# Three-layer graph network, one core: built blocks and one-hots moved inside the windows of layers 1 and 2, the dense tiles of layer 3 on two banks, the self edge put into the blocks

## The reference

```python
loops = jnp.arange(n)
src = concatenate([src, loops]); dst = concatenate([dst, loops])
norm_edge = dinv[src] * dinv[dst]
for W, b in ((W1, b1), (W2, b2), (W3, b3)):
    h = relu(segment_sum((h @ W)[src] * norm_edge[:, None], dst) + b)
x = layernorm(x + h)
```

## Time and profile before

| what | us |
|---|---|
| median of 3 runs | 2859.15 (2855.75 to 2860.95) |
| the profiled execution's own time | 2853.73 |
| its span, first to last instruction | 2851.4 |
| PE busy | 2381.7 |
| POOL busy | 1900.6 |
| DVE busy | 1013.9 |
| ACT busy | 539.5 |

### The profile page before, as it was taken

The page is one execution under the profiler, slowest core; times in us unless marked ns, Lnnn a source line. Parts: engine busy times, 40 slices in busy tenths (PEclk is TensorE's granted clock), DMA queues, the critical chain, the costliest instruction groups (busy, mean ns, idle before and its releaser), DMA issues.

```text
span 2851.4 us, 37925 instructions
## 1 busy us (share of the span) xinstructions
PE 2381.7 (84%) x11284; PEld 1529.4 (54%) x11285; DVE 1013.9 (36%) x1370; ACT 539.5 (19%) x1322; POOL 1900.6 (67%) x1996
## 2 busy tenths in 40 slices
PE   7887777777777778888888888888988898989897
PEld 6754555555555555443443434343446677777676
DVE  8733434444344343332222222222222323232322
ACT  6412332333333323221101111111110000000000
POOL 4377776777777776767777777777776555555543
PEclk9799999999999999999999999999998999999898
DMA  6344545554554554877777777777775545454543
GB/s 188 126 120 145 165 145 157 162 162 149 166 163 138 168 162 138 255 231 230 231 227 232 226 232 228 231 228 229 231 224 183 170 144 179 139 182 139 176 133 100
DMA packets 195418, 515.59 MB, mean 181 GB/s; under 512 B 39468, under 2 KB 87203, under 8 KB 189251
## 3 DMA queue, kind: packets, MB, share of 16 engines
q0 software_dynamic: 120240, 362.54, 43.6%
q1 hardware_dynamic: 69171, 111.99, 11.6%
q10 hardware_dynamic: 5984, 40.77, 3.9%
HBM read 444.05 MB, written 71.09 MB: 181 GB/s over the span
## 4 chain that ended last, share of the span: by engine, by line
PE 49%; POOL 17%; issue 14%; DMA 9%; DVE 5%; POOLq 3%; ACT 1%; DVEq 0%; ACTq 0%; SPq 0%
PE ps_acc L1229 21%; POOL rows L559 17%; PE ps_T L1298 15%; DMA rows<-table,idx 9%; PE ps_o L1265 6%; POOLq L568 3%; PE ps_acc L1227 2%; DVE works L893 1%; PE ps_d L1174 1%; PE ps_e L1286 1%; PE ps_l L1286 1%; DVE acc L827 1%; PE ps_h L1252 1%; PE ps_d L1252 1%; ACT parts L1088 1%
## 5 line engine op out<-in xcount | busy, mean ns | idle before, releaser
L559 POOL DMA_INDIRECT rows<-table,idx x1955 | 1855.2, 949 | 839.0 <-issue 703.2
L1229 PE MATMUL ps_acc<-rows,sel 128*128 128x256 f32 (+2 forms) x3948 | 1455.6, 486 | 314.1 <-DMA rows<-table,idx 220.4
L1229 PEld LDWEIGHTS ps_acc<-rows,sel 128*128 128x128 f32 x3948 | 689.4, 197 | 774.0 <-DMA rows<-table,idx 379.5
L827 DVE TENSOR_TENSOR acc<-ps_acc,acc 128x256 f32<-128x256 f32 (+1 forms) x123 | 65.3, 531 | 1119.2 <-PE ps_acc L1229 1119.2
L746 DVE SCALAR_TENSOR_TENSOR sel<-ps_e,firsts,dstT 128x1152 f32<-128x1152 f32 x242 | 342.7, 1416 | 0.0
L1265 PE MATMUL ps_o<-w,hT 128*128 128x512 f32 (+1 forms) x784 | 270.5, 488 | 0.8 <-ACT hT L1051 0.8
L745 DVE COPY idx<-srcT 128x9 int32 (+1 forms) x242 | 45.7, 189 | 634.0 <-PE ps_acc L1229 631.4
L1298 PE MATMUL ps_T<-parts,rows 128*128 128x256 bf16 x1764 | 240.2, 285 | 25.9 <-DVE agg L852 25.9
L1298 PE MATMUL ps_T<-parts,works 128*128 128x256 bf16 x1764 | 234.7, 281 | 23.8 <-DVE agg L852 23.8
L1071 ACT ACTIVATE made<-ps_o,dinv 128x512 f32<-128x512 f32 (+1 forms) x98 | 56.8, 580 | 900.3 <-PE ps_o L1265 900.3
L1298 PEld LDWEIGHTS ps_T<-parts,rows 128*128 128x128 bf16 x1764 | 179.4, 102 | 81.8 <-issue 34.8
(11 more groups left out here) (174 smaller groups left out, 1303.2 us busy)
## 6 DMA issues: line engine op xcount, KB each, us to landing
built<-parts SPq DMA_DIRECT2D x24, 1568.0 KB, 6.5
rows<-table,idx POOLq DMA_INDIRECT x1955, 2.9
works<-built ACTq DMA_DIRECT2D x12, 1568.0 KB, 6.9
rows<-built ACTq DMA_DIRECT2D x12, 1568.0 KB, 6.8
table<-made SPq DMA_DIRECT2D x49, 256.0 KB
acc<-table SPq DMA_DIRECT2D x49, 256.0 KB
acc<-table SPq DMA_DIRECT2D x74, 128.0 KB
table<-parts SPq DMA_DIRECT2D x7, 896.0 KB, 8.7
```

Of the source, the lines that this page charges most:

```text
L559: pool.indirect_dma_start(out=rows_of[phase][:, k, 0:WIDTH[phase]], out_offset=None, in_=table[phase][0:nodes, :], in_offset=bass.Indirect ...
L827: v.tensor_tensor(acc[:, 0:w], ps_acc[:, 0:w], acc[:, 0:w], ALU.add).then_inc(sum_taken, 1)
L1229: ins = mm(ps_acc[:, 0:w], sel[:, k, :], first if k == 0 else rows_of[phase][:, k, 0:w], start=(k == 0), stop=(k == ORDER[-1]))
```

## The change

1. **Layer 1, DVE.** `one_hots` moves ahead of `take_sum` in the same window. The windows with one-hots are written out in groups of four.
2. **Layer 1, PE.** The eight pairs of a half move from positions 10 to 17 to positions 1 to 8, ahead of the hidden layer and the product. In the last window of layer 1 they start at position 5. The first four building windows of layer 2 take the places of the other windows of layer 2, with the product at the end.
3. **Layer 1, ACT.** Four of the eight copies of a half come right after `scale`, the other four after the turned tile's copy, all ahead of `made` (but in one window, where they stay at the end).
4. **Self edge.** DVE adds the identity to the diagonal block of each built tile in `making` (`add_self`), 24 times, and SP stores the block row after that. SP's store of a block row stands one tile later in its queue: three of them (before: two) now stand behind windows of layer 2. `take_dense`, SP's loads of the dense tiles' own rows and their semaphores are gone.
5. **Layer 3.** The dense tiles use two banks in turn, ps_T and ps_h; the normalization reads the bank itself. The 147 matmuls are spread over 18 positions instead of 17, the first six of them ahead of slot 0.

The diff, cut to its core:

```diff
-        ps_dense = ps_T
+        ps_dense = [ps_T[:, 0:C], ps_h[:, 0:C]]
...
                     def store_built(j, of):
-                        sp.wait_ge(pair_kept, 2 * PAIRS * (j + 1) + 2)
+                        sp.wait_ge(self_added, j + 1)
...
-                    def dense_rows(j, n, first=False):
-                        if not first:
-                            sp.wait_ge(acc_d_used, j)
-                        sp.dma_start(acc_d, table[2][bass.ds((GATHER + j) * P, P), :]).then_inc(own_d_in, 16)
+                    def dense_residual(j, n, first=False):
...
-                        with sp.Fori(0, (T - BUILT_FROM) // 4) as i:
+                        rows_and_store(BUILT_FROM)
+                        with sp.Fori(0, (T - BUILT_FROM) // 4 - 1) as i:
                             for b in range(4):
-                                rows_and_store(BUILT_FROM + 4 * i + b)
+                                rows_and_store(BUILT_FROM + 4 * i + b + 1)
                                 if b % 2 == 1:
                                     store_built(2 * i + b // 2, b // 2)
+                        for b in range(3):
+                            rows_and_store(T - 3 + b)
+                            if b == 1:
+                                store_built(DENSE - OVER // 2 - 2, 0)
                         store(T - 1)
                     elif phase == 1:
-                        for b in range(OVER):
+                        for b in range(OVER + 1):
                             rows_and_store(1 + b)
-                            if b % 2 == 1:
-                                store_built(DENSE - OVER // 2 + b // 2, b // 2)
-                        with sp.Fori(OVER + 1, T) as t:
+                            if b % 2 == 0:
+                                store_built(DENSE - OVER // 2 - 1 + b // 2, 1 - b // 2 % 2)
+                        with sp.Fori(OVER + 2, T) as t:
...
-            def take_dense(j):
+            def finish_dense(j, into, seq):
                 v_.wait_ge(dense_done, j + 1)
-                v_.wait_ge(own_d_in, 16 * (j + 1))
-                v.tensor_tensor(acc_d, ps_dense[:, 0:C], acc_d, ALU.add).then_inc(dense_taken, 1)
-            def finish_dense(j, seq):
-                v_.wait_ge(dense_taken, j + 2)
-                normalize(acc_d, GATHER + j, acc_d_used, j + 1, res_d, res_d_in, j, seq, y3_d, y3_d_free, y_d_ready)
+                normalize(ps_dense[into], GATHER + j, dense_taken, j + 3, res_d, res_d_in, j, seq, y3_d, y3_d_free, y_d_ready)
+            def add_self(j, of):
+                v_.wait_ge(pair_kept, 2 * PAIRS * (j + 1) + 2)
+                its = making[of][:, bass.ds(GATHER + j, 1), :].rearrange("p a d -> p (a d)")
+                v.tensor_tensor(its, its, ident[:, :], ALU.add).then_inc(self_added, 1)
...
             def one_window():
-                def steady(phase, t):
+                def steady(phase, t, hots=None, whole=None):
                     n = nth(phase, t)
                     base = base_of(t)
                     prepare(n, t, base, 0)
+                    if whole is not None:
+                        add_self(*whole)
+                    if hots is not None:
+                        one_hots(hots)
...
                 v_.wait_ge(key_kept, len(key_banks))
-                with v_.Fori(BUILT_FROM, T) as t:
-                    steady(0, t)
-                    one_hots(t - BUILT_FROM)
+                def four(i, first, phase, whole=True):
+                    for b in range(4):
+                        steady(phase, first + b, 4 * i + b,
+                               None if b % 2 or not whole and b == 0 else (2 * i + b // 2 - 1, 1 - b // 2))
+                        if phase == 1 and b > 0:
+                            split(b - 1)
+                four(0, BUILT_FROM, 0, False)
+                with v_.Fori(1, (T - BUILT_FROM) // 4) as i:
+                    four(i, BUILT_FROM + 4 * i, 0)
                 to_next(0)
-                steady(1, 1)
-                one_hots(T - BUILT_FROM)
-                with v_.Fori(2, OVER + 1) as t:
-                    steady(1, t)
-                    one_hots(T - BUILT_FROM - 1 + t)
-                    split(t - 2)
-                with v_.Fori(OVER + 1, T) as t:
+                four((T - BUILT_FROM) // 4, 1, 1)
+                steady(1, OVER + 1, None, (DENSE - 1, 1))
+                split(OVER - 1)
+                with v_.Fori(OVER + 2, T) as t:
...
                 finish(0, nth(2, 0) + 2, 0)
-                with v_.Fori(2, GATHER) as t:
+                def pair(t, into):
                     steady(2, t)
-                    take_dense(t - 2)
                     finish(t - 1, nth(2, t) + 1, of_gather(t - 1))
-                    finish_dense(t - 2, of_dense(t - 2))
+                    finish_dense(t - 2, into, of_dense(t - 2))
+                with v_.Fori(0, DENSE // 2 - 1) as i:
+                    for into in range(2):
+                        pair(2 * i + into + 2, into)
+                pair(GATHER - 1, 0)
                 n = nth(2, GATHER)
                 take_sum(2, n - 1, n - 1, True)
-                take_dense(DENSE - 1)
                 finish(GATHER - 1, n + 1, of_gather(GATHER - 1))
-                finish_dense(DENSE - 1, of_dense(DENSE - 1))
+                finish_dense(DENSE - 1, 1, of_dense(DENSE - 1))
...
-            def tile(phase, t, per):
+            def tile(phase, t, per, built_half=None, at_end=False):
                 n = nth(phase, t)
                 scale(phase, t, per)
+                def keep(*gs):
+                    if built_half is not None:
+                        keep_pairs(*built_half, range(*gs))
+                if not at_end:
+                    keep(0, PAIRS // 2)
                 if phase == 0:
                     act.wait_ge(turned, n + 1)
                     nc.scalar.activation(aggT[:, 0:C], ps_T[:, 0:C], ACT.Copy).then_inc(aggT_ready, 1)
+                    if not at_end:
+                        keep(PAIRS // 2, PAIRS)
...
                         relu_T(ps_T[:, m * P:(m + 1) * P], b2T, m)
+                    keep(PAIRS // 2, PAIRS)
                 w = WIDTH[phase + 1]
                 act.wait_ge(o_done, n + 1)
                 act.wait_ge(made_free, n + 1)
                 act.sem_inc(act_step, 1)
                 nc.scalar.activation(made[:, 0:w], ps_o[:, 0:w], ACT.Copy, scale=dinv[:, bass.ds(t, 1)]).then_inc(made_ready, 1)
+                if at_end:
+                    keep(0, PAIRS)
...
-            def keep_half(i, j, of, part):
-                for g in range(PAIRS):
+            def keep_pairs(i, j, of, part, gs):
+                for g in gs:
...
-                with act.Fori(0, (T - BUILT_FROM) // 4) as i:
+                def four(i, first, phase):
                     for b in range(4):
-                        tile(0, BUILT_FROM - 1 + 4 * i + b, 1)
-                        keep_half(4 * i + b, 2 * i + b // 2, b // 2, b % 2)
+                        tile(phase, first + b, 1, (4 * i + b, 2 * i + b // 2, b // 2, b % 2),
+                             isinstance(i, int) and phase == 0 and b == 3)
+                FOURS = (T - BUILT_FROM) // 4
+                with act.Fori(0, FOURS - 1) as i:
+                    four(i, BUILT_FROM - 1 + 4 * i, 0)
+                four(FOURS - 1, T - 5, 0)
                 tile(0, T - 1, 1)
-                for b in range(OVER):
-                    tile(1, b, 1)
-                    keep_half(2 * DENSE - OVER + b, DENSE - OVER // 2 + b // 2, b // 2, b % 2)
+                four(FOURS, 0, 1)
...
-            pe.sem_inc(dense_taken, 1)
+            pe.sem_inc(dense_taken, 2)
...
-                        ins = mm(ps_dense[:, 0:C], counts_of, parts[:, h, i, :], start=(h == 0 and i == 0),
+                        ins = mm(ps_dense[into], counts_of, parts[:, h, i, :], start=(h == 0 and i == 0),
...
-                def building(i):
+                def building(i, start=1):
                     def beside(k):
                         at = ORDER.index(k)
-                        if at >= SLOTS - PAIRS:
-                            build(i, at - (SLOTS - PAIRS))
+                        if start <= at < start + PAIRS:
+                            build(i, at - start)
                     return beside
                 def with_dense(i, into):
                     def beside(k):
                         at = ORDER.index(k)
-                        if at > 0:
-                            dense(i, into, range((at - 1) * T // (SLOTS - 1), at * T // (SLOTS - 1)))
+                        dense(i, into, range(at * T // SLOTS, (at + 1) * T // SLOTS))
...
-                steady(0, T - 1, LAST_PLACES[0], building(T - 1 - BUILT_FROM))
+                steady(0, T - 1, LAST_PLACES[0], building(T - 1 - BUILT_FROM, LAST_PLACES[0][2] + 1))
                 turn(0, T - 1)
                 hidden(T - 1)
                 product(0, T - 1)
                 first_window(1)
                 with pe.Fori(1, OVER + 1) as t:
```

(2 more changed lines are left out.)

11 lines of the change are left out of this document (5 added, 6 removed).

## The result

The changed kernel takes 2713.64 us, the median of 4 runs (2711.35 to 2715.84). The kernel before took 2860.05 us beside it (4 runs, 2855.75 to 2867.82). The ratio is 0.9485, with a 95% interval of 0.9463 to 0.9508. The forecast of 2730 us, faster, holds; it was 16 us too high. The profiled execution took 2715.02 us with a span of 2712.8 us, against 2851.4 before: 138.6 us less.

A forecast was written before the change was run, and what follows sets the result against it. POOL's gather pace was taken to bound layer 2 and nearly layer 1, PE layer 3. Gains of 104 and 30 less 5 make 129 us off 2853.7, 2724.7, given as 2730 us for the median; range 2705 to 2770.

The forecast's parts named there:

- Layer 3, 104 us: Layer 3: two banks and six early dense matmuls cut a step from 28.34 to 23.84 us, 104 us in all.
- The bank's wait and the clock behind it, 88 us in the sum: Layer 3: PE's wait for the single bank and work at 1.2 GHz cost 3.84 us a step, 23 steps.
- the six matmuls: Layer 3: six dense matmuls ahead of slot 0 hide in PE's wait for the gathered sum, 0.66 us a step.
- Two rivals: Layer 3: the clock stays low, 2769 us, chance 0.06; the second bank gives nothing, 2834 us, chance 0.03.
- Layer 1, 30 us: Layer 1: earlier pairs and copies remove most of POOL's waits for indices, 30 us, between 0 and 38.
- The rival that layer 1 gives nothing: Layer 1: POOL waits as long as before, because of the later store and early one-hots; 2760 us, chance 0.12.
- POOL's 37.8 us of waits: Layer 1: POOL's waits for indices beyond plain gaps, laid to PE's 58.0 us for copies and one-hots.
- DVE's one-hots ahead of the sum, 0: Layer 1: the added DVE work ahead of the sum costs 0, with 3 us of cover.
- The rival on the other side: Layer 1: one-hots on DVE hold up the sum, up to 273 us over 48 windows; 3033 us, chance 0.03.
- Layer 2's first windows, +5: Layer 2's start: a third store falls into this stretch and adds 5 us, between -11 and +11.
- the 11.5 us of excess: Layer 2's first windows: time above POOL's pace before the change, charged to two stores at 5.7 us each.
- three places where POOL stands: Layer 2's first five windows: POOL was to stand three times for no named reason, about 17 us above its pace.

## Why the prediction was right, and where it was not

**Layer 3, 104 us: right, by its own mechanism.** The trace gives 106.1 us, the single bank put back 102. A step was to be 24.50 - 0.66 = 23.84 us and is 23.84. The bank's wait and the clock behind it, 88 us in the sum, come to some 86, if the six matmuls are worth the same on every chip; these, 0.66 a step in the sum, come to 0.7 or 0.8 on the slower chips, the only ones that ran them apart. Two rivals fall with this: the clock came back to 1.00, and the second bank was what the dense tile waited for. POOL kept the pace. The Trainium skill (TensorE: Matmul & The Clock Gate, section "HAM oscillation — how this bites in real kernels") tells of a kernel that, with its loop put right, gained nothing further from double-buffering PSUM. In this case the second bank and the six early matmuls together give 102 of 2860 us.

**Layer 1, 30 us: the size right, the reason shown in part.** Between gathers 100 and 767 it is 31.2 us, and in the two other kernels with the new order, one bank and stores earlier, 30.3 and 33.6. The rival that layer 1 gives nothing is out. The step that failed is the one that put POOL's 37.8 us of waits down to PE's 58 us for copies and one-hots alone, because the one was larger than the other. With 54.0 us of the waits for copies put back, 10 us return and not 30. And 36.1 of the 37.8 us stood 20 to 30 us behind a store of a block row, for which the sum had left 4 us. What was right is that the new order rids POOL of its waits: it does so with the stores in their old place too, at 841.05 us. That the size came out so near is in part luck, since the later stores, priced at nothing in layer 1, may remove most of the same waits by themselves.

**DVE's one-hots ahead of the sum, 0: right, and for the reason given.** The sum waits 84.2 us for PE in 42 windows, 2 us each and 1.2 at the least, where I had said 3 us of cover. The rival on the other side was priced at 273 us for 48 windows. The kernel with late pairs and early one-hots shows it at 217, with the addition of the self edge as part of it. What kept it away is what the prediction named: the last half's pairs are done at position 8.

**Layer 2's first windows, +5: not borne out.** The changed kernel shows 4.1 us less than before, not 5 more. Neither is firm. Five executions have 100.0 us (before), 95.9, 95.4, 97.9 and 101.2 (one bank, the same instructions there as in the changed kernel). Two executions of the same code lie 5.4 us apart, so a term of this size can't be read from one trace of each kernel. Two steps failed. The third store does not fall into this stretch but behind it, at gather 874, and adds nothing that the next stretch shows (865.16 us, before 864.97). And the 11.5 us of excess went to two stores in even shares, when no run had moved a store. There are three places where POOL stands, as I wrote, two of them with DVE's indices as the named reason (2.34, 1.09 and 1.16 us beyond plain), but they make 4.6 us and not 17.

**The sum.** 129 us forecast, 138.6 by the spans, 146.4 by the medians of 4 runs. The difference to the spans is 7.5 us ahead of layer 3 (32.5 for 25; layer 2's term alone is 9.1 and layer 1's 1.2, and what lies between takes 2.8 back), and 2.1 in layer 3. The spans and the medians differ because the kernel before's profiled execution, 2853.73 us, lies below all its other runs, and I had seen 5.4 us of that.

## What to carry to other kernels

In this kernel the wait for a single bank cost the wait and the low clock behind it; where a trace shows such a wait, price both from a step in which the wait is absent, if the trace has one. A producer and a consumer in a ring of engines that wait for each other are best moved together: early matmuls with early one-hots, or late with late, differ by 5 to 9 us here, and either one alone costs over 200. And when a wait is to be charged to a cause, the size of the cause is no proof: put the cause back alone, and see how much returns. Do so with the other changes in and with them out, since two changes can remove the same wait.

## What the runs showed that I had not expected

**A lower clock that costs little.** In the changed kernel layer 1 runs at a granted clock of 0.93, lower than the 0.97 before, and is faster. PE now waits for rows once or so in two windows, and works at the lower level behind it:

```profile
650.76 1.22 PE L1257 MATMUL ps_acc<-rows,sel 128*128 128x256 f32 x2 [4.72 <-DMA rows<-table,idx]
651.78 0.53 PE L1314 MATMUL ps_l<-works 128*128 128x196 bf16 x2
652.10 1.11 PE L1257 MATMUL ps_acc<-rows,sel 128*128 128x256 f32 x2
```

From 650 to 660 the clock is 0.66, from 660 to 680 it is 1.00 again. POOL keeps its pace of 1.25 us up to 660 and then stands 2.6 us beyond plain in two gathers; over all of gathers 100 to 767 such standing is 9.3 us. POOL sets the pace of this stretch, so the lower clock can have cost it no more than these.

**Slower chips, another kernel.** On the two chips where all took 28% longer a gather has the same 0.95 us on POOL and the same median pace of 1.25, and the median one-hot on DVE and `made` on ACT last as long. But the engines stand, several us at a time, with nothing that the profile names: in the chain of waits of the seven runs there 34 to 48% is "another core or an unknown queue", and in the changed kernel and the one-bank kernel on quicker chips it is not among the largest shares. Changes that are read from the waits of one chip don't carry over: late one-hots cost 246 us on a quicker chip, while on chip 4 their ratio, 0.9582, lies beside 0.9568 for the dense matmuls from position 1. The cause stays open.
